# A deformable convolution woven into a selective scan: two of three taps of the first group go from VectorE to ScalarE, and the third turn of a tile moves ahead of the branch on TensorE

## What is computed

```python
# layer 0: nine taps (n) for each pixel, each the weighted sum of four corners
def corner(yc, xc, wgt):
    valid = (yc >= 0) & (yc < Hv) & (xc >= 0) & (xc < Wv)
    v = gather(x, clip(yc), clip(xc))              # 128 channels at one pixel
    return v * (wgt * valid)[:, None]
samp = corner(y0i, x0i, wy0 * wx0) + corner(y0i, x0i + 1, wy0 * wx1) \
     + corner(y0i + 1, x0i, wy1 * wx0) + corner(y0i + 1, x0i + 1, wy1 * wx1)
samp = samp * mask[:, None]
out = einsum('bcnhw,ocn->bohw', samp, w_conv)
# layer 1: the scan, for four directions k, 256 inner channels and 16 states
h = exp(dt_l * A) * h + (dt_l * x_l) * b_l
y = einsum('bkdn,bkn->bkd', h, c_l)
```

## Time and profile before

| what | value |
|---|---|
| median of 3 runs | 16272.06 us (16271.22 to 16283.77) |
| profiled execution | 16293.11 us, its span 16291.1 us |
| TensorE busy | 12767.1 us, 78% of the span |
| VectorE busy | 11114.6 us, 68% |
| ScalarE busy | 9636.9 us, 59% |
| GpSimd busy | 5728.3 us, 35% |
| mean granted TensorE clock | 0.793 of full speed |

### The profile page before, as it was taken

One profiled execution on the slowest core, in us unless ns is written; L12 is line 12 of the kernel. 1 busy time (PEld: TensorE's weight loads), 2 busy tenths in 40 slices (PEclk: granted clock), 3 DMA queues, 4 the chain that ended last, 5 costly groups with the idle time before them and its releaser, 6 DMA issues.

```text
span 16291.1 us, 179969 instructions
## 1 busy us (share of the span) xinstructions
PE 12767.1 (78%) x47232; PEld 7840.2 (48%) x47232; DVE 11114.6 (68%) x12535; ACT 9636.9 (59%) x20979; POOL 5728.3 (35%) x4760
## 2 busy tenths in 40 slices
PE   5777878788787878878778787877878778787835
PEld 4454554545445454554545445454453545545412
DVE  3585875848668485784848758486684857848585
ACT  1375674747657375674756647476574756747433
POOL 6451441514325052350614415143250523516100
PEclk7878778787887978779787787878879687797857
DMA  5442332423334242342423324233341423424100
GB/s 162 117 131 70 115 110 76 130 78 106 89 95 127 61 124 72 113 121 62 133 71 112 107 78 129 77 106 90 97 128 60 127 71 112 119 67 130 54 1 13
DMA packets 662468, 1563.83 MB, mean 96 GB/s; under 512 B 76952, under 2 KB 347484, under 8 KB 650556
## 3 DMA queue, kind: packets, MB, share of 16 engines
q0 software_dynamic: 368640, 1208.25, 25.9%
q1 hardware_dynamic: 289980, 302.80, 6.2%
q10 hardware_dynamic: 2304, 33.56, 0.5%
HBM read 1338.15 MB, written 206.14 MB: 95 GB/s over the span
## 4 chain that ended last, share of the span: by engine, by line
PE 42%; DVE 23%; DVEq 14%; issue 9%; ACT 6%; DMA 2%; POOL 2%; ACTq 1%; SPq 0%; POOLq 0%
PE psum L1253 6%; PE psum L1132 6%; DVEq L897 6%; PE psum L1066 5%; DVE arena L901 4%; PE psum L1262 4%; PE psum L1076 3%; DVEq L889 3%; PE psum L1085 2%; DVE arena L906 2%; DVE arena L868 2%; DVE arena L872 2%; DVE arena L870 2%; DVE arena L923 2%; DVEq L877 2%
## 5 line engine op out<-in xcount | busy, mean ns | idle before, releaser
L636 POOL DMA_INDIRECT gathered<-cell_table,index x2880 | 3243.1, 1126 | 2971.3 <-PE psum L1066 1957.0
L636 POOL DMA_INDIRECT arena<-cell_table,index x1440 | 1992.7, 1384 | 2083.7 <-PE psum L1066 1787.5
L1076 PE MATMUL psum<-samples_t,pack 128*128 128x128 f32 x9216 | 1861.6, 386 | 273.3 <-ACT samples_t L423 273.3
L423 ACT COPY samples_t<-psum 128x384 f32<-128x384 f32 x1536 | 716.7, 467 | 2228.6 <-PE psum L1066 1980.6
L1165 PE MATMUL psum<-arena,pack 32*128 32x512 f32 x1024 | 844.9, 917 | 1463.3 <-DVEq L920 1463.3
L1076 PEld LDWEIGHTS psum<-samples_t,pack 128*128 128x128 f32 x9216 | 1738.0, 291 | 463.2 <-ACT samples_t L423 463.2
L1066 PE MATMUL psum<-pack,gathered 128*128 128x128 f32 x11520 | 1572.5, 296 | 442.2 <-DVE gathered L810 288.2
L1066 PEld LDWEIGHTS psum<-pack,arena 128*128 128x128 f32 x6912 | 1324.8, 216 | 1057.7 <-issue 1056.9
L1066 PE MATMUL psum<-pack,arena 128*128 128x128 f32 x6912 | 1536.9, 408 | 360.6 <-DVE arena L992 241.7
L436 ACT ACTIVATE arena<-arena,weight 128x128 f32<-128x128 f32 x5760 | 1734.5, 390 | 6.9 <-DMA arena<-cell_table,index 6.7
L436 ACT ACTIVATE gathered<-gathered,weight 128x128 f32<-128x128 f32 x5760 | 1730.2, 389 | 1.7 <-DMA gathered<-cell_table,index 1.4
(11 more groups left out here) (164 smaller groups left out, 21064.7 us busy)
## 6 DMA issues: line engine op xcount, KB each, us to landing
cell_table<-arena SPq DMA_DIRECT2D x64, 2112.5 KB
gathered<-cell_table,index POOLq DMA_INDIRECT x2880, 3.8
arena<-in_x SPq DMA_DIRECT2D x16, 2048.0 KB, 7.6
image<-in_x SPq DMA_DIRECT2D x16, 2048.0 KB, 7.8
x_dram<-image SPq DMA_DIRECT2D x16, 2048.0 KB, 10.2
arena<-x_dram SPq DMA_DIRECT2D x16, 2048.0 KB, 7.8
out<-arena ACTq DMA_DIRECT2D x16, 2048.0 KB, 7.2
arena<-cell_table,index POOLq DMA_INDIRECT x1440
```

Source lines behind the costliest of these rows:

```text
L636: pool.indirect_dma_start(gathered[m][:, n * CORNERS * C:(n + 1) * CORNERS * C], None, table, bass.IndirectOffsetOnAxis(ap=index[:, at:at ...
L1076: last = pe.matmul(psum[:, V_BANK, 0:TILE], wt("wconv")[:, n * C:(n + 1) * C], samples_t[:, n, :], start=n == 0, stop=n == TAPS - 1)
```

## The change

Three things change. `BY_ACT` becomes (0, 1, 2), so ScalarE takes part in group 0 too: VectorE weighs its first tap (`TAPS_V` = 1, 4 corners, 512 elements), ScalarE the other two (8 corners, 8 instructions), ahead of group 1. The turn of group 0 waits for both. And the turn of the third group is no longer issued by TensorE in the next unit, but in its own one, between the flag's matmul and the wait for the flag.

```diff
-BY_ACT = (1, 2)
+BY_ACT = (0, 1, 2)
+TAPS_V = 1
...
-                for at in range(GT * CORNERS):
+                for at in range(0 if m else TAPS_V * CORNERS, GT * CORNERS):
...
                     if with_next:
+                        weigh(b + 1, t, 0)
                         weigh(b + 1, t, 1)
...
-                corners = gathered[m].rearrange("p (n k) -> p n k", k=C)
-                w4 = weight4[:, bass.ds(t * TAPS + m * GT, GT), :].rearrange("p n (c o) -> p (n c) o", o=1)
-                v.tensor_mul(corners, corners, w4.broadcast_to([128, GT * CORNERS, C])).then_inc(S["weighted_v"], 1)
+                corners = gathered[m][:, 0:TAPS_V * CORNERS * C].rearrange("p (n k) -> p n k", k=C)
+                w4 = weight4[:, t * TAPS + m * GT:t * TAPS + m * GT + TAPS_V, :].rearrange("p n (c o) -> p (n c) o", o=1)
+                v.tensor_mul(corners, corners, w4.broadcast_to([128, TAPS_V * CORNERS, C])).then_inc(S["weighted_v"], 1)
...
-                elif m in BY_ACT:
-                    pe.wait_ge(S["weighted_a"], ((a - 1) * TILES + t) * len(BY_ACT) + m - BY_ACT[0] + 1 + SEED["weighted_a"])
                 else:
-                    pe.wait_ge(S["weighted_v"], ((a - 1) * TILES + t) * (GROUPS - len(BY_ACT)) + m + 1)
+                    if m == 0:
+                        pe.wait_ge(S["weighted_v"], (a - 1) * TILES + t + 1)
+                        own_wait(pe)
+                    pe.wait_ge(S["weighted_a"], ((a - 1) * TILES + t) * GROUPS + m + 1 + SEED["weighted_a"])
...
                         if not is_(t, 0):
-                            turn(b + 1, t - 1, 1 - par, 2)
                             convolve(b + 1, t - 1)
...
                     pe.matmul(psum[0:1, V_BANK, 0:1], one[:, 0:1], fast[:, :], start=True, stop=True).then_inc(S["flag_psum"], 1)
+                    if with_next:
+                        turn(b + 1, t, par, 2)
                     pe.wait_ge(S["flag_set"], unit + 1)
...
-                    turn(b + 1, TILES - 1, 1, 2)
                     convolve(b + 1, TILES - 1)
```

## The result

| | before | after |
|---|---|---|
| median, us | 16271.64 | 17388.92 |
| runs, lowest to highest | 16255.99 to 16283.77 | 17384.56 to 17391.03 |
| profiled span, us | 16291.1 | 17382.5 |
| mean granted clock of TensorE, share of full | 0.793 | 0.787 |
| VectorE busy, share of the span | 68% | 61% |

The changed kernel takes 1.0687 times as long, with a 95% interval of 1.0668 to 1.0705: 1117 us more, where 837 were forecast. The time is inside the range given, 280 us above the forecast value. Most of this part is about those 280 us, because the wait that makes the loss appeared in another place than the one forecast.

What follows compares the result with a forecast made beforehand. The prediction took VectorE's own queue to bound a unit. It added 532 us of waiting at the flag and 305 us from the moved turn, 837 us in all, for 17110 us, with a range from 16740 to 17470.

Steps and rivals of the forecast that it cites:

- VectorE is the bound, and saves 1.07 us: VectorE's own queue paces a unit; L810 shrinks from 1536 to 512 elements, 1.07 us less a unit.
- ScalarE's eight activations cost 2.34 us and reach the flag: +532 us: Ahead of group 1's weighing: L910 comes 1.38 us later in even units, 0.89 in odd, 532 us in all.
- some tenths, inside the same lateness: Third group's copy and the decays on ScalarE, behind the moved turn: a small delay, given no term of its own.
- L910 waiting in nearly every unit: Expected sign in the profile: VectorE waits there for the flag, 2 us and more, some 900 us in all.
- The moved turn makes every second unit late: +305 us: TensorE reaches the end of the next unit's turn 1 late; 305 us taken between estimates of 225 and 385.
- 3.31 from L1165 to the next line's start: TensorE's time in an even unit from L1165 to the convolution's start, part of a 13.59 us stretch.
- But the rest is tight: TensorE's queue through the next unit's turn 1 ends 1.84 us late in an even unit; B still comes in time.
- the rival with the branch: TensorE's load and branch run only after the moved turn: 1.5 us more, +349 us, 17460; chance 0.11.
- the forecast case: Flag wait and late moved turn together: 17110 us, within 16990 to 17230; chance 0.50.
- The clock: TensorE idles more, so turn 1 takes 2.79 us at half clock, not 1.50: 17404 us; chance 0.14.
- Chain alone: Only ScalarE's chain counts and TensorE is never late: +420 us, 16690, or else 16800; chance 0.17.
- The turn should start 0.3 us after the weighing: Expected sign on TensorE: the moved turn starts 0.3 us after group 2 is weighed.

Runs made afterwards that it cites:

- split_only: Changed kernel with the third group's turn back in the next unit, ahead of the convolution; ScalarE still weighs two taps of group 0: 16971.9 us.
- warm: Changed kernel with 20 matmuls that serve nothing in TensorE's wait ahead of the third turn: 16815.1 us.
- turn_only: Kernel before with only the third group's turn moved ahead of the branch, VectorE weighing all three taps of group 0: 16775.6 us.
- one_tap: Changed kernel with one tap of group 0 on ScalarE and two on VectorE: 17084.9 us.
- flag_early: Changed kernel with the flag's matmul ahead of the turns of groups 0 and 1: 17473.3 us.
- load_first: Changed kernel with TensorE's load of the flag ahead of the third turn, compare and branch behind it: 17401.0 us.
- after_branch: Changed kernel with the third turn behind TensorE's branch, still in its own unit: 17027.0 us.
- free2: Kernel before with one tap on ScalarE, the flag's matmul ahead of turns 0 and 1, the add behind the flag, third group's copy behind the decays: 16069.5 us.

## Why the prediction was right in the sign and short in the size

*VectorE is the bound, and saves 1.07 us.* Right, in size (L812 0.692 us for a forecast 0.69) and in what it means: in the changed kernel all of it is waiting.

*ScalarE's eight activations cost 2.34 us and reach the flag: +532 us.* Right in the mechanism, and to 0.01 us in a single unit (L912 at T+14.09, period 18.79). The size was too small for this half alone: split_only costs 675 us. What the sum lacked there is the copy of the third group, which holds up the decays and with them ScalarE's whole chain (T+4.42 for T+3.91); the prediction named this copy only beside the moved turn, as "some tenths, inside the same lateness". warm is 543 us slower than before, near the 532, but at another clock than the kernel before, and the starts of its units account for 479 of them; so that nearness is partly luck. But in the changed kernel this wait is not what VectorE mostly stands in: 205 us and not 900, since in a long unit the add has already cost more than the flag would. The line "L910 waiting in nearly every unit" under what would show it was wrong, and would have been right of split_only (850.9 us in 480 units).

*The moved turn makes every second unit late: +305 us.* Right in the mechanism, that a late stretch of TensorE carries into the next unit and that short and long units then alternate; wrong in size: 479 us in turn_only, and 574 by what warm takes away, against 305. The term that was mis-sized is "3.31 from L1165 to the next line's start". It was read from a unit before the change, in which the branch was already over and the matmuls of B took 0.66 us. In the changed kernel the means over the 136 even units of more than 20.2 us are 0.92 us of pause from the turn's end to L1168 and 3.85 us from there to the convolution (L1168 at the lower level takes 1.19 us): 4.77 for 3.31. In 83 odd units of more than 21.2 us it is 0.88 and 4.13, 5.01 for 4.03. The turn (2.79), the convolution (4.02 and 3.87 for 4.21) and the turn's start (T'+1.21 in the unit shown, for T'+1.14) were sized well, though in the mean of the 136 the turn starts earlier, at T'+0.48.

The place was wrong too, and that step is the one from "is in time" for B to "But the rest is tight", which has turn 1 as the only rest. The small add, L817, was named only as a part of VectorE's work. It waits for the convolution, and ahead of the flag's cast VectorE has the scans behind it: from the add to the cast 4.33 us in the long even units and 5.04 in the odd ones (of more than 21 us, in which the add waited), 4.48 and 5.19 from the convolution's end. By turns 0 and 1 the flag's matmul starts 3.62 and 3.87 us after the convolution's end, and a cast 0.22 later. So VectorE comes later by the add, by 0.6 us in an even unit and 1.1 in an odd one, and the wait shows at L819. With the lengths that the forecast had, 3.28 + 0.98 + 0.22 = 4.48 behind the convolution, even units would have come out the same by either way; the odd ones would not.

The pause is the rival with the branch, which had 1.50 us and a chance of 0.11: it was partly true, and came on top of the forecast case, not in its place. That B would then come just late is seen too: L888 waits 1.56 us in the long unit shown, and 63.8 us in all, in 92 units.

*The clock.* The rival had turn 1 at half clock in every unit. It took under 1.6 us in 459 of the 465 units, the short unit shown has its flag at the time forecast for turn 1 at full clock, and the mean clock hardly moved (0.793 to 0.787). But the sum took the lengths at the lower level as given. Since the loop is made of TensorE's time at that level, the clock decides how much it costs: warm takes 574 us off. I had put the clock against the wrong instruction, turn 1, and not against the turn that was moved behind the long wait.

*Chain alone, 16690 to 16800.* The change doesn't give it; warm comes close (16815), with the clock up.

*The sum.* 837 us were added up from 532 and 305, and each half by itself measured more (675 and 479), while both at once cost 1117 and not their sum of 1154. So both terms were short, and the forecast was 25% under the loss.

*The turn should start 0.3 us after the weighing.* 0.39 us (2952.19 to 2952.58). The copy L424 ends about then too and is what the profile names as the releaser. Which of both it is stays open.

*The last image unchanged.* Right, 496.8 us.

What is shown, then: that each half costs by itself (split_only, turn_only), that the cost follows the number of activations (turn_only, one_tap), that the flag's place doesn't set the pace of the changed kernel (flag_early), that most of the lateness goes when TensorE's clock is up (warm), and that the pause behind the turn belongs to the branch's place and not to the load (load_first, after_branch). Argued only: that drains are the pause, why single pauses reach 1.9 us, and how the 574 us of warm divide between the loop and what a higher clock would give any of these kernels.

## What to carry to other kernels

When a piece of one engine's queue moves later, list every instruction of the other engines that waits for anything behind it, the small ones too, and ask of each how far from it the end of the period is; the add of 0.29 us was the costly one here. Where periods alternate, the pace is a loop over two of them, and a wait taken out of one comes back in the other, so cost the whole loop before moving a wait. Shifting work from a full engine to one with gaps pays by how much of it fits into the chain that the next stage waits for: here, with the flag and the add moved, four activations did and eight did not.

## What the hardware showed that was not expected

Idle matmuls paid here. Twenty matmuls of 128 columns (4.73 us at 2.4 GHz), put into 6 us in which TensorE waited anyway, raised its mean granted clock from 0.787 to 0.928 and took 574 us off (17388.9 to 16815.1); ten of them in free2 raised it from 0.820 to 0.883 for 111 us. Twelve transposing matmuls behind them took 1.50 us at 2.4 GHz and 2.79 at 1.2 GHz without them.

A branch on TensorE that stands behind a queued turn leaves 0.88 us between that turn's end and the first matmul behind the branch (465 times, 409.4 us), whether the flag is loaded ahead of the turn or behind it. With the turn behind the branch the pause is gone. In this kernel a branch costs least where its engine waits anyway.
